# Cross-attention, first batch: its context loaded at once into a weight buffer, its halves split among other engines, weight halves and statistics spread over the softmax

## The reference, cut to what matters

```
e = layernorm(x)                                          # encoder rows, 512 x 512 a batch
Sim = (e @ w1)[:, :, None] + (ctx @ w2)[:, None, :] + einsum('bid,bjd->bij', e * w3, ctx) + b_sim
A = softmax(Sim, axis=2);  h = A @ ctx
Batt = softmax(max(Sim, axis=2), axis=1);  hc = Batt @ e
x1 = x + tanh(g) * (concat([e, h, e * h, e * hc]) @ W_qv + b_qv)
```

## Time and profile before

| | |
|---|---|
| median of 3 runs | 1283.96 us (1283.77 to 1284.76) |
| the profiled execution's own time | 1281.38 us |
| its span, first to last instruction | 1279.6 us |
| PE busy | 1216.1 us, 95% |
| DVE, ACT, POOL busy | 833.4, 643.4, 661.8 us |
| first 25.93 us: PE busy | 11.60 us |
| 25.93 to 32.76 us: PE busy | 0.00 us |
| 32.76 to 48.78 us: PE busy | 10.99 us |

### The profile page before, as it was taken

The page is one execution under the profiler, slowest core; times in us unless marked ns, Lnnn a source line. Parts: engine busy times, 40 slices in busy tenths (PEclk is TensorE's granted clock), DMA queues, the critical chain, the costliest instruction groups (busy, mean ns, idle before and its releaser), DMA issues.

```text
span 1279.6 us, 19762 instructions
## 1 busy us (share of the span) xinstructions
PE 1216.1 (95%) x6376; PEld 909.9 (71%) x6376; DVE 833.4 (65%) x1531; ACT 643.4 (50%) x1418; POOL 661.8 (52%) x483
## 2 busy tenths in 40 slices
PE   3899999999999999698999999999999999999995
PEld 2688888888888888565767667666767667677653
DVE  5577777777686946274665765675664755756655
ACT  4443434434343431466556556556556656665551
POOL 2634242424243433349396395595593791873972
PEclk9799999999999999799999999999999999999998
DMA  6231413142322313301002002011020011010010
GB/s 232 81 116 50 123 41 123 41 123 66 98 83 90 96 72 110 130 1 34 1 5 96 0 16 82 0 35 63 0 66 33 0 66 33 0 66 0 10 55 34
DMA packets 40714, 75.74 MB, mean 59 GB/s; under 512 B 3760, under 2 KB 4272, under 8 KB 40688
## 3 DMA queue, kind: packets, MB, share of 16 engines
q1 hardware_dynamic: 40688, 75.42, 17.9%
HBM read 58.63 MB, written 16.78 MB: 59 GB/s over the span
## 4 chain that ended last, share of the span: by engine, by line
PE 48%; DVE 5%; POOL 3%; ACT 1%; issue 1%; DVEq 0%; POOLq 0%; ACTq 0%
PE ps_r L1573 11%; PE ps_o L1646 8%; PE ps_s L1633 8%; PE ps_s L1625 7%; PE ps_r L1585 5%; PE ps_r L1608 5%; DVE z L1360 2%; POOL v_acc L1165 2%; DVE z_tmp L1349 1%; POOL spare L1159 1%; PE ps_r L1599 1%; PE ps_r L1592 1%; PE ps_r L1562 1%; DVE nmax L1329 1%; DVE q L1387 0%
## 5 line engine op out<-in xcount | busy, mean ns | idle before, releaser
L1177 POOL TENSOR_TENSOR z<-z,z_tmp 128x1280 f32<-128x1280 f32 x40 | 117.1, 2926 | 199.9 <-DVE z_tmp L1349 197.8
L1329 DVE TENSOR_REDUCE nmax<-ps_s 128x1 f32<-128x512 f32 x256 | 163.5, 680 | 85.7 <-PE ps_s L1625 84.7
L1225 ACT ACTIVATE pt<-ps_s 128x512 f32<-128x512 f32 x256 | 139.1, 595 | 144.8 <-PE ps_s L1633 144.5
L1216 ACT ACTIVATE probs<-ps_s,nmax 128x512 f32<-128x512 f32 x256 | 174.1, 693 | 16.0 <-DVE nmax L1329 15.9
L1165 POOL TENSOR_TENSOR v_acc<-v_acc,spare 128x512 f32<-128x512 f32 x128 | 172.8, 1350 | 10.0
L1159 POOL TENSOR_TENSOR spare<-xv,pick 128x512 f32<-128x512 f32 x128 | 142.2, 1111 | 10.0
L1633 PEld LDWEIGHTS ps_s<-ident,probs 128*128 128x128 f32 x1024 | 109.5, 141 | 48.7 <-issue 40.8
L1633 PE MATMUL ps_s<-ident,probs 128*128 128x128 f32 x1024 | 140.3, 280 | 1.3 <-ACT probs L1216 1.2
L1625 PE MATMUL ps_s<-k,q 64*128 64x512 f32 x768 | 123.6, 426 | 3.7 <-ACT pt L1225 3.7
L1646 PE MATMUL ps_o<-pt,v_acc 128*64 128x512 f32 x512 | 116.9, 598 | 0.7 <-ACT pt L1225 0.7
L226 POOL TENSOR_TENSOR e_t<-e_t 128x512 fp32r<-128x512 f32 x32 | 40.3, 1299 | 147.4 <-ACT e_t L432 147.4
(11 more groups left out here) (167 smaller groups left out, 2136.4 us busy)
## 6 DMA issues: line engine op xcount, KB each, us to landing
stage<-in_x SPq DMA_DIRECT2D x32, 256.0 KB, 3.2
stage<-in_ctx SPq DMA_DIRECT2D x32, 256.0 KB, 2.7
x_sb<-in_x SPq DMA_DIRECT2D x8, 1024.0 KB, 5.3
x_dram<-x_sb SPq DMA_DIRECT2D x32, 256.0 KB, 2.0
stage<-x_dram SPq DMA_DIRECT2D x8, 1024.0 KB, 5.6
spare<-x_dram SPq DMA_DIRECT2D x8, 1024.0 KB, 5.6
out_dram<-spare SPq DMA_DIRECT2D x32, 256.0 KB, 2.1
stage<-in_ctx_t SPq DMA_DIRECT2D x28, 256.0 KB, 2.9
```

The source lines that it names most:

```text
L1177: pool.tensor_tensor(zv, zv, z_tmp[:, h % 2], ALU.add).then_inc(z_pool, 1)
L1216: act.activation(probs[:, n % BANKS, :], ps_s[:, n % BANKS, :], ACT.Exp, bias=nmax[:, n:n + 1], accum_out=den[:, h, t:t + 1]).then_inc(p_e ...
L1225: act.activation(pt[:, h % 4, :, t * P:(t + 1) * P], ps_s[:, n % BANKS, :].rearrange("p (k t) -> p k t", k=NT), ACT.Copy).then_inc(pt_read ...
L1329: dve.tensor_reduce(nmax[:, n:n + 1], ps_s[:, n % BANKS, :], AX_X, ALU.max, negate=True).then_inc(nmax_ready, 1)
```

## The change

Only the first batch's opening is rewritten. The context is loaded at once into `weh_raw`, which was free, so its load waits for nothing; the weight block that was there before is loaded once POOL has taken the context's lower halves. SP's order of the first loads is another, and the constants have semaphores of their own. Next x is loaded into `stage` when turning and row dots are done. POOL takes over from DVE the lower halves of the transposed context. ACT takes the upper halves of the transposed context ahead of its copies of e, and spreads the upper halves of `wh` and of `e_t` through the softmax; those of `weh` come after it. DVE takes two row dots before the scaling instead of after, puts the statistics of the next batch's x one by one into the softmax, and puts the last ten parts of their `root` behind the softmax.

```diff
             def stage_loaded(eng, b, t, use):
-            eng.wait_ge(slot_loaded[t], b * (3 * 16) + use * 16)
+            eng.wait_ge(slot_loaded[t], b * (3 * 16) + use * 16 - 16)
...
+        def ctx_source(eng, b, t, first):
+            if first:
+                eng.wait_ge(c0_loaded[t], 16)
+                return weh_raw
+            stage_loaded(eng, b, t, 2)
+            return stage
...
             load_x(0, True)
-            sp.dma_start(w1_row[:], w_sim[0:D].partition_broadcast(P)).then_inc(const_loaded, 16)
-            sp.dma_start(w_cols[:], w_sim_cols).then_inc(const_loaded, 16)
-            sp.dma_start(gate_raw[:], g_xattn.partition_broadcast(P)).then_inc(const_loaded, 16)
-            sp.dma_start(bsim_col[:], b_sim.partition_broadcast(P)).then_inc(const_loaded, 16)
-            sp.dma_start(bias_row[:], b_qv.partition_broadcast(P)).then_inc(const_loaded, 16)
+            sp.dma_start(w_cols[:], w_sim_cols).then_inc(cols_loaded, 16)
             load_first_ctx_t()
+            sp.dma_start(w1_row[:], w_sim[0:D].partition_broadcast(P)).then_inc(dots_loaded, 16)
+            sp.dma_start(bsim_col[:], b_sim.partition_broadcast(P)).then_inc(dots_loaded, 16)
+            load_first_ctx()
+            sp.dma_start(gate_raw[:], g_xattn.partition_broadcast(P)).then_inc(bias_loaded, 16)
+            sp.dma_start(bias_row[:], b_qv.partition_broadcast(P)).then_inc(bias_loaded, 16)
             sp.dma_start(wh_raw[:], w_blocks[1]).then_inc(wh_loaded, 16)
-            sp.dma_start(weh_raw[:], w_blocks[2]).then_inc(weh_loaded, 16)
-            load_first_ctx()
+            load_x(1, second=True)
             sp.wait_ge(ct_lo, ND)
             load_residual(0)
-            load_x(1)
+            sp.wait_ge(c_lo, NT)
+            sp.dma_start(weh_raw[:], w_blocks[2]).then_inc(weh_loaded, 16)
...
-            ctx_lo(0)
-            for n in range(2 * ND):
-                pool.wait_ge(w_hi, n + 1)
-                take_lo(pool, *((wh, n, wh_raw) if n < ND else (weh, n - ND, weh_raw))).then_inc(w_lo, 1)
+            for k in range(ND):
+                pool.wait_ge(ct_hi, k + 1)
+                take_lo(pool, c_t2, k, x_sb).then_inc(ct_lo, 1)
+            ctx_lo(0, True)
+            weight_lo(wh, wh_raw, 0)
+            rows_lo(0)
+            weight_lo(weh, weh_raw, ND)
...
+            def first_softmax():
+                softmax_exp(0, 0)
+                weights_hi(wh, wh_raw, wh_loaded, (0, 1))
+                softmax_exp(0, 1)
+                probs_hi(0, 0)
+                weights_hi(wh, wh_raw, wh_loaded, (2, 3))
+                softmax_exp(0, 2)
+                probs_hi(0, 1)
+                rows_hi(0, (0, 1))
+                softmax_exp(0, 3)
+                probs_hi(0, 2)
+                rows_hi(0, (2, 3))
+                probs_hi(0, 3)
+                weights_hi(weh, weh_raw, weh_loaded, range(ND))
...
+            def first_front():
+                for k in range(ND):
+                    ctx_t_hi(0, k, True)
+                for t in range(NT):
+                    copy_e(0, t)
+                for k in range(ND):
+                    scaled_e_hi(0, k)
+                act.wait_ge(bias_loaded, 2 * 16)
+                act.activation(gate[:], gate_raw[:], ACT.Tanh).then_inc(gate_ready, 1)
+                ctx_hi(0, True)
...
+            def first_softmax():
+                row_max(0, 0)
+                row_stats(1, 0)
+                normalise(0, 0)
+                row_max(0, 1)
+                row_stats(1, 1)
+                probs_lo(0, 0)
+                normalise(0, 1)
+                row_stats(1, 2)
+                row_stats(1, 3)
+                row_max(0, 2)
+                probs_lo(0, 1)
+                normalise(0, 2)
+                for part in range(4):
+                    root(1, part)
+                row_max(0, 3)
+                probs_lo(0, 2)
+                normalise(0, 3)
+                row_totals(0)
+                probs_lo(0, 3)
+                row_totals_max(0)
+                for part in range(4, ROOT_PARTS):
+                    root(1, part)
...
-            dve.wait_ge(const_loaded, 5 * 16)
+            dve.wait_ge(dots_loaded, 2 * 16)
+            for t in range(2):
+                row_dot(0, t)
             front(0, True)
```

More of the change, by code:

```diff
@@ L161, in cross_attention @@
         bias_ready = sem("bias_ready")
+        c0_loaded = [sem(f"c0_loaded{t}") for t in range(NT)]
         ct0_loaded = [sem(f"ct0_loaded{k}") for k in range(ND)]
@@ L248, in _, with load_x @@
         def _(sp):
-            def load_x(b, first=False):
+            def load_x(b, first=False, second=False):
                 for t in range(NT):
-                    if not first:
+                    if second:
+                        sp.wait_ge(et_ps, t + 1)
+                        sp.wait_ge(ew1_ready, t + 1)
+                    elif not first:
                         sp.wait_ge(c_lo, b * NT - NT + t + 1)
@@ L350, in rest @@
                     take_lo(pool, e_t2, k, e_t).then_inc(et_lo, 1)
+            def rest(b):
                 for k in range(ND):
@@ L394, in scaled_e_hi, with ctx_hi, weights_hi, rows_hi @@
                 act.activation(es_t2[:, 0, k, :], tmp[:, k, :], ACT.Copy).then_inc(es_hi, 1)
-            def ctx_hi(b):
+            def ctx_hi(b, first):
                 for t in range(NT):
-                    stage_loaded(act, b, t, 2)
-                    cast_hi(act, c_2, t, stage).then_inc(c_hi, 1)
-            def weights_hi(pair, raw, loaded):
+                    cast_hi(act, c_2, t, ctx_source(act, b, t, first)).then_inc(c_hi, 1)
+            def weights_hi(pair, raw, loaded, tiles):
                 act.wait_ge(loaded, 16)
-                for k in range(ND):
+                for k in tiles:
                     cast_hi(act, pair, k, raw).then_inc(w_hi, 1)
+            def rows_hi(b, tiles):
+                for k in tiles:
+                    act.activation(e_t2[:, 0, k, :], e_t[:, k, :], ACT.Copy).then_inc(et_hi, 1)
             def softmax_exp(b, t):
@@ L430, in attended @@
                     act.wait_ge(feat_ps, b * NT)
-                for k in range(ND):
-                    act.activation(e_t2[:, 0, k, :], e_t[:, k, :], ACT.Copy).then_inc(et_hi, 1)
+                    rows_hi(b, range(ND))
                 for k in range(ND):
@@ L520, in scaled_e_lo, with row_dots @@
                 take_lo(dve, es_t2, k, tmp).then_inc(es_lo, 1)
-            def row_dots(b):
-                for t in range(NT):
+            def row_dots(b, begin=0):
+                for t in range(begin, NT):
                     row_dot(b, t)
@@ L531, in front @@
                 dve.wait_ge(et_copied, b * NT + NT)
+                if first:
+                    dve.wait_ge(cols_loaded, 16)
                 scaled_e(b, 0, first)
@@ L535, in front @@
                         scaled_e(b, k + 1, first)
-                    ctx_t_lo(b, k, first)
+                    if not first:
+                        ctx_t_lo(b, k)
                     scaled_e_lo(b, k)
@@ L562, in probs_lo, with row_totals, row_totals_max, softmax @@
                                   a_t2[:, 0, :, t * P:(t + 1) * P].bitcast(F32), ALU.subtract).then_inc(at_lo, 1)
-            def softmax(b, first, more):
-                stats_after = {1: (0, 1), 2: (2, 3)} if first else {0: (0, 1), 1: (2, 3)}
-                root_after = {2: range(4), 3: range(4, ROOT_PARTS)} if first else {2: range(7), 3: range(7, ROOT_PARTS)}
+            def row_totals(b):
+                dve.wait_ge(nmax_ready, b * NT + NT)
+                dve.wait_ge(ew1_biased, b + 1)
+                dve.scalar_tensor_tensor(mtot[:], nmax[:], -1.0, ew1[:], ALU.mult, ALU.add).then_inc(b_dve, 1)
+            def row_totals_max(b):
+                dve.wait_ge(b_dve, b * 6 + 1)
+                dve.reduce_max(pmax[:], mtot[:], AX_X).then_inc(b_dve, 1)
+            def first_softmax():
[21 more added lines that the diff above has]
+                    root(1, part)
+            def softmax(b, more):
+                stats_after = {0: (0, 1), 1: (2, 3)}
+                root_after = {2: range(7), 3: range(7, ROOT_PARTS)}
                 row_max(b, 0)
@@ L585, in softmax @@
                     probs_lo(b, t)
-                    if t == 0 and not first:
+                    if t == 0:
                         residual(b - 1, 2)
-                    if t == 1 and not first:
+                    if t == 1:
                         x1_row_stats(b - 1, 2)
-                dve.wait_ge(b_dve, b * 6 + 1)
-                dve.reduce_max(pmax[:], mtot[:], AX_X).then_inc(b_dve, 1)
+                row_totals_max(b)
             def row_share(b, k):
```

58 lines of the change are left out of this document (26 added, 32 removed).

## The result

The changed kernel takes 1285.16 us (median of 20 runs, 1283.34 to 1287.07), the kernel before 1283.08 us beside it (20 runs). The ratio is 1.0017 with a 95% interval of 1.0009 to 1.0024: it is slower, by about 2.2 us (1.2 to 3.1). The forecast was -0.1 us.

What follows compares the result with a forecast made beforehand. PE, busy nearly without gap from 65.89 us, was taken to pass the opening's savings or losses to the end. First exponential -3.9 and softmax +3.8 gave -0.1 us on 1283.96: 1283.9 us, range 1276.5 to 1287.5.

Steps and rivals of the forecast that it cites:

- What bounds the kernel: From 65.89 to 570 us PE is busy 491.41 of 504.11 us, so what the opening saves or loses passes on.
- the landmark: Start of the second `attend` product, 53.34 us in the kernel before; what follows was taken as the same in both kernels.
- Opening, +4.0: Before `normalise_x`: four Newton instructions on DVE held beside POOL's transposed context, start at 14.1 instead of 10.04 us.
- Front, 9.7: From the start of `normalise_x` to the last half of the scaled e: 9.7 us instead of 12.1, ending at 23.8.
- The rest up to the row maximum: ... one wait for POOL: Two dots 1.2, two bias instructions 0.7, one POOL wait 0.9: maximum at 26.6, first exponential at 27.3, 3.9 us sooner.
- Softmax, +3.8: From first exponential to second `attend`, 22.1 us before: terms 0.5 - 1.0 + 1.0 + 1.9 + 1.4 sum to +3.8.
- C: Rival: POOL hardly disturbs, ACT's lateness was all; exponential at 22.5 or so, 1273.5 us; chance 0.10.
- theory C: Theory tested by the runs: pauses bring PE down to 1.2 GHz, and that takes the gain.
- A: Rival and forecast: the waits on POOL eat the gain, 1282.1 to 1285.4 us; chance 0.50.
- B: Rival: only wide instructions wait, Newton chains slip between POOL's; 1278 us, range 1276 to 1281; chance 0.22.
- D: Rival: POOL waits plus PE at 1.2 GHz for the fourth scores and second `attend`, +4.1, 1288.0 us; chance 0.18.
- P: Theory tested by the runs: POOL's subtractions hold DVE's SBUF instructions, each place costing what its waits add up to.

Runs made afterwards that it cites:

- run 1: Changed kernel, POOL's lower halves of the transposed context waiting until all four `normalise_x` are done: 1282.99 us, ratio 0.9990 to the kernel before.
- run 2: Changed kernel, each POOL subtraction of the transposed context done twice: 1289.15 us, ratio 1.0041 to the kernel before.
- run 6: Changed kernel, POOL writing the transposed context's lower halves with memset instead of subtracting: 1281.60 us, ratio 0.9986 to the kernel before.
- run 3: Changed kernel, the transposed context's lower halves back on DVE: 1283.01 us, ratio 0.9989 to the kernel before.
- run 8: Changed kernel, POOL's context halves waiting until DVE has scaled `bias_row`: 1283.28 us, ratio 1.0001 to the kernel before.
- run 4: Changed kernel, POOL's lower halves of `weh` waiting until the Newton chain is through: 1284.13 us, ratio 1.0001 to the kernel before.
- run 5: Changed kernel with all three POOL waits, those of run 1, run 4 and run 8: 1279.16 us, ratio 0.9965 to the kernel before.
- run 7: Kernel before, with only the context's early load into `weh_raw` and the loads that follow from it: 1284.28 us, ratio 1.0007 to the kernel before.
- run 9: Kernel before, with run 7's early context load and run 8's POOL wait behind `bias_row`: 1281.91 us, ratio 0.9994 to the kernel before.
- run 10: Run 5, fourth row maximum ahead of the first seven Newton instructions, POOL's `e_t` halves behind those of `weh`: 1277.76 us, ratio 0.9961 to the kernel before.

## Why the prediction was wrong

**What bounds the kernel**: right. The opening decides: the landmark moved by +2.36 us (53.34 to 55.70), the third `attend` by 3.93, and with that the 3.8 us of the span are there. "What follows it is the same in both kernels" was wrong by 1.6 us: the second product of `attend` itself.

**Opening, +4.0**: right, +4.4 measured, 0.3 of it x being there later. Casts from 7.37, POOL from 8.08 (8.1 said), four Newton instructions held, `normalise_x` at 14.44 (14.1 said). Runs 1 and 2 show the cause, by taking it away (9.91) and doubling it (18.34).

**Front, 9.7**: right, 14.44 to 24.13 is 9.69.

**"The rest up to the row maximum: ... one wait for POOL"**: this is the step that failed. One wait of 0.9 was put down and three came, 3.1 us; the maximum was at 29.05, not 26.6, and of that 2.4 the opening had brought 0.3. The exponential was 1.5 us sooner, not 3.9. The rows for it were at hand: POOL needs 5 us for the context, and what DVE had to do meanwhile was one instruction after the other on SBUF. The paragraph on the Trainium skill had it nearer. The Trainium skill's page "SBUF — State Buffer", section "Who interferes with whom", counts DVE instructions with two SBUF inputs among those that contend with a GpSimd instruction that reads SBUF, tensor-scalar forms among those that can, and reductions never. The trace agrees in all three: row dot 1.77 us for 0.69, bias addition 1.14 for 0.23, and the row maximum at 0.68 beside POOL. I had let it add one wait, to a sum of its own. The same section of the Trainium skill says that a GpSimd instruction that only writes SBUF doesn't contend with a DVE instruction with two SBUF inputs. Run 6 agrees, 0.16 to 0.17 us beside memset.

**Softmax, +3.8**: right in its sum, 25.94 us from first exponential to second `attend` against 25.9 said, and in most of its terms; that it came out to the tenth is partly luck, as errors of 0.1 to 0.5 us cancel. The first `normalise` was not held (0, +0.5 said: it fell into POOL's pause between 30.24 and 31.13). From the turning of tile 0 to that of tile 1 it was -0.8 (-1.0 said); the third scores, 4.58 us for 5.06, are 0.5 of it. From the turning of tile 1 to that of tile 2 it was +0.9 (+1.0 said), to that of tile 3 +2.0 (+1.9), and the first `attend` to the second +1.7 (+1.4).

**Rivals** (the prediction's letters; its C is not theory C above). A's mechanism is what happened, and 1285.16 lies within its bounds. (The bounds were added to 1283.96; from 1283.9 they would be 1282.0 and 1285.3.) B is refuted by the rows of the opening; C by the same. D was half right: not the fourth scores, which took 3.02 us, but the second `attend`, 4.60 for 2.99, +1.6 us. PE's granted clock is 0.50, the 1.2 GHz level, from 55.70 to 59.00 and 0.95 from there to 60.27, after 1.64 us of idle time ahead of `gmax`'s product. In run 2 that idle time is 1.68 us and the product takes 4.59; in runs 1, 3, 6 and 8 it is 0.56 to 0.83 us and the product 3.00 to 3.04, and in run 4 there is none and it takes 3.02. So the length of the pause goes with the level. That it makes it was not tried by itself, since in those runs the clock also rose at another place in the first product (5.15 to 5.46 us there, 4.35 and 4.31 here). So theory C holds for 1.6 us of the loss at most, and P for the rest. The clock costs in the good runs too. In runs 5, 7, 9 and 10 the first product takes 5.18 to 5.46 us, where it took 4.33 before, and there PE hardly waits for `gmax`, so 0.9 to 1.1 us go straight into the start of the second. So the step that failed and D's half together make the miss: +2.4 ahead of the row maximum and +1.6 from the clock, 4.0 at the third `attend`, for the +3.9 by which the span misses the forecast. The bound that stood in A (+1.4 for a row dot and the bias) was nearer to what happened than the value taken.

**Where the gain went**: the early context does free ACT (runs 5 and 9 show 5 to 7 us at the exponential). It was handed to POOL, which starts as soon as its data are there, and so lay beside DVE's chains at three places. By the ratios holding POOL back at `c_t` is worth 3.5 us by itself, at `weh` 2.0 and at `c` 2.0, each uncertain by 1.6 to 1.8 us; at all three 6.7 (4.9 to 8.4). In `c_t`, in `weh` and in `c` the 1.6 us of the second `attend` are had each time, but they can be had only once; against that, a wait taken away can show up again one instruction on, as in run 8. The early context by itself was not shown to be worth anything (run 7, +0.9 us with an interval from -0.4 to 2.1), for which the halves of `weh` on ACT are as much the reason as POOL.

**What stays open**: by the ratio the time moved by 2.2 us and in the profiled execution by 3.85; that of the kernel before lay 1.7 us under its median of 20. The account above is of these two executions. Single runs of one kernel lie up to 6 us apart, and from the start of the `wec` products to the end the profiled executions took between 1202.1 and 1205.7 us, with no order by kernel; PE's granted clock falls to 1.2 GHz at slightly different places there. What sets these places wasn't tried.

## What to carry to other kernels

When a load is moved up, ask which engine will start on it unasked, and lay that engine's whole stretch beside the other's chain: for four POOL instructions of 128x512 that read and write SBUF count three or four waits of about 1.0 us, as long as DVE has SBUF work there (4 of 4 in the Newton chain, 3 of 4 at the context), and not one wait in all. A wait of POOL's on a semaphore that is set behind the chain costs a line; three of them gave back 6.7 us here. Then look for the next engine in the way: in runs 7 and 9 it was ACT, standing for a weight load ahead of an exponential. A longer chain of tiny instructions is the worst neighbour: 0.19 us a step becomes 1.2.

## What the runs showed of the hardware

- A DVE instruction of 128x4, 0.16 us by itself, takes 1.13 to 1.21 us beside back-to-back POOL subtractions, and exactly one gets in for each of them (4 of 4, and 8 of 8 with twice as many).
- POOL waits as well: beside DVE's row dots four of its subtractions took 7.93 us, beside instructions on 128x4 tiles 4.94, as with DVE idle for the most part (4.93, in the kernel before from 26.25 on).
- POOL's memset of 128x512 (0.52 us) held the one tensor-scalar instruction on DVE that fell beside it, 0.40 for 0.17 us; those with two inputs took 0.16 to 0.17 us beside the other three.
- DVE's maximum from PSUM (0.68 us) and its row statistics (0.68 us, one SBUF input) take the same time beside POOL's subtractions as without them.
- PE's second product of `attend` ran for the most part at 1.2 GHz (4.60 and 4.59 us) behind pauses of 1.64 and 1.68 us, and at 2.4 GHz (3.00 to 3.04 us) behind pauses of 0 to 0.83 us. The pause was not tried by itself.
